# Cross-attention scores of L2 and L3 as 64-row products in two PSUM banks

## What is computed

```python
# L2: biases on q, k, v, o; x is layer-normalised first, the result is added to x
Q = (q @ w_q.T + b_q).reshape(B, Sq, 16, 16).transpose(0, 2, 1, 3)
scores = einsum('bhqd,bhkd->bhqk', Q, K) / sqrt(16)
attn = softmax(scores, axis=-1)
out = einsum('bhqk,bhkd->bhqd', attn, V) -> (B, Sq, 256) @ w_o.T + b_o
# L3: no biases, but a distance bias for each head, a mask, and 1 + sum in the denominator
scores = einsum('bhqd,bhkd->bhqk', Q, K) * scale - slopes[h] * (query_pos - key_pos)
scores = where(mask == 0, -inf, scores)
e = exp(scores - max);  attn = e / (1 + sum(e))
```

## Time and profile before

| | |
|---|---|
| median of 3 runs | 2059.65 us (2058.97 to 2062.86) |
| profiled execution, its own time | 2075.04 us |
| its span, first to last instruction | 2073.2 us |
| mean granted TensorE clock | 0.874 of full speed |
| TensorE busy with products | 1637.2 us, 79% of the span |
| VectorE busy | 1118.5 us, 54% |
| ScalarE busy | 757.3 us, 37% |

### The profile page before, as it was taken

How to read it: one execution, slowest core, us unless ns; L and a number is a source line. 1 busy time by engine, 2 the same in 40 slices (tenths; PEclk the granted TensorE clock), 3 DMA queues, 4 the chain that set the end, 5 groups by cost and what they waited for, 6 DMA issues and landing times. The chain is left out here.

```text
span 2073.2 us, 31829 instructions
## 1 busy us (share of the span) xinstructions
PE 1637.2 (79%) x9560; PEld 1217.6 (59%) x9561; DVE 1118.5 (54%) x2571; ACT 757.3 (37%) x1808; POOL 479.3 (23%) x485
## 2 busy tenths in 40 slices
PE   5965999999999999999998549479544489845993
PEld 4752666666666666666666449358432257634993
DVE  3326565566666666666665620357766846561222
ACT  1211445555445545444542113134344123301331
POOL 1002221222222222222221043211132400006421
PEclk9977999999999999999996569779766589857997
DMA  5001000000000000000003131250100000012203
GB/s 207 0 0 48 1 1 0 0 0 0 0 21 28 1 1 0 0 0 0 1 1 122 41 129 47 96 211 0 31 1 0 0 3 0 0 41 77 64 32 129
DMA packets 25874, 69.19 MB, mean 33 GB/s; under 512 B 6107, under 2 KB 13421, under 8 KB 23756
## 3 DMA queue, kind: packets, MB, share of 16 engines
q1 hardware_dynamic: 19756, 53.35, 7.0%
q0 software_dynamic: 6048, 14.99, 2.3%
HBM read 51.07 MB, written 18.78 MB: 34 GB/s over the span
## 5 line engine op out<-in xcount | busy, mean ns | idle before, releaser
L1062 PE MATMUL banks<-l_ffn_h2T,l_ffn_w 128*128 128x128 f32 (+1 forms) x1536 | 184.0, 278 | 32.2 <-ACT l_ffn_h2T L1175 32.2
L1062 PEld LDWEIGHTS banks<-l_ffn_h2T,l_ffn_w 128*128 128x128 f32 (+1 forms) x1536 | 172.7, 181 | 42.7 <-issue 38.9
L987 PE MATMUL banks<-l_ffn_in_wqkv,l_ffn_hT 128*128 128x512 f32 x384 | 192.2, 611 | 1.9 <-issue 1.1
L1155 ACT ACTIVATE l_ffn_work<-banks,l_ffn_att_bias,l_ffn_att_scale 128x256 f32<-128x256 f32 x256 | 140.5, 567 | 52.2 <-DVE l_ffn_att_bias L1296 52.2
L1009 PE MATMUL banks<-l_ffn_kT,l_ffn_qT 128*128 128x512 f32 x256 | 133.1, 602 | 0.0
L258 POOL TENSOR_TENSOR rstd<-mean_var,neg_half 128x1 f32 (+1 forms) x80 | 46.0, 575 | 350.8 <-DVE mean_var L251 350.7
L1295 DVE TENSOR_REDUCE l_ffn_att_top<-banks 128x2 f32<-128x512 f32 x128 | 88.5, 692 | 62.6 <-PE banks L1009 62.6
L1185 ACT ACTIVATE l_ffn_gate<-banks,l_ffn_layer_cols 128x128 f32<-128x128 f32 x192 | 59.7, 362 | 135.6 <-PE banks L1062 135.6
L1071 PE MATMUL banks<-l_ffn_in_w,l_ffn_ff 128*128 128x256 f32 (+1 forms) x384 | 99.6, 388 | 0.0
L946 POOL TENSOR_TENSOR l_ffn_rden_wide<-l_ffn_att_rden,ones 128x512 f32<-128x512 f32 x32 | 33.2, 1039 | 282.1 <-DVE l_ffn_att_rden L1307 282.1
L2040 DVE COPY l_route_c_all<-l_ffn_in_w 128x1024 f32 x39 | 30.7, 787 | 123.7 <-PE banks L1973 86.9
(11 more groups left out here) (383 smaller groups left out, 3738.6 us busy)
## 6 DMA issues: line engine op xcount, KB each, us to landing
l_experts_rows<-l_experts_pairs SPq DMA_DIRECT2D x16, 512.0 KB, 7.7
l_ffn_in_w<-in_L_w SPq DMA_DIRECT2D x2, 4096.0 KB, 20.4
l_ffn_in_down<-in_L_down SPq DMA_DIRECT2D x1, 4096.0 KB, 14.3
l_experts_c_rows<-l_route_c_all SPq DMA_DIRECT2D x2, 2048.0 KB, 7.6
l_experts_pairs<-l_experts_rows SPq DMA_DIRECT2D x4, 1024.0 KB, 10.5
l_ffn_in_wqkv<-in_L_wqkv SPq DMA_DIRECT2D x1, 3072.0 KB, 12.3
l_ffn_w<-in_L_w SPq DMA_DIRECT2D x2, 1364.0 KB, 7.1
x_res<-in_x SPq DMA_DIRECT2D x4, 512.0 KB, 5.5
```

The lines of the kernel that those rows point to most:

```text
L987: mm = pe.matmul(ps[:, m.bank + 1 + n, :], hT[:, m.b, m.odd, ch, 1 - ch:P + 1 - ch], wqkv[:, bass.ds(m.layer, 1), ch, n * INNER:(n + 1) * ...
L1062: mm = pe.matmul(ps[0:FW[j], m.bank + j // 2, to:to + P], w1[:, ch, at:at + FW[j]], h2T[:, ch, m.b, :], start=(j % 2, n, ch) == (0, 0, 0), ...
L1155: ex = nc.scalar.activation(work[:, m.b, slot, :], ps[:, m.bank + slot // 2, (slot % 2) * 2 * P:(slot % 2 + 1) * 2 * P], ACT.Exp, bias=bia ...
```

## The change

In each half of the channels a group of 64 rows (four heads) becomes a product of its own. Group 0 (partitions 0 to 63) writes bank 4b+2, group 1 (partitions 64 to 127) bank 4b+3; each product has 64 rows, 128 stationary columns and 256 moving columns, and a bank holds 256 columns from each half of the channels. `keys` is half as wide: 4 heads for each row group, selected by `own_quarter`. In L3 the mask and the distance bias are written into both banks first, then the four key products are added. The heads thus stand in another order in the score banks; `head_of` puts the mix back in place, and V1 is laid out to fit.

```diff
+        own_quarter = sb("own_quarter", [P, QUARTER])
-        keys = sb("keys", [P, DCH, BATCH, HALF_XH, CTX])
+        keys = sb("keys", [P, DCH, BATCH, QUARTER, CTX])
...
+                v.tensor_tensor(own_quarter[:], own_head[:, 0:QUARTER], own_head[:, QUARTER:], ALU.add)
...
-                        v.tensor_tensor(keys[:, half, b, :, :], keysT[:, half, b, :].unsqueeze(1).broadcast_to((P, HALF_XH, CTX)),
-                                        own_head[:].unsqueeze(2).broadcast_to((P, HALF_XH, CTX)), ALU.mult)
+                        v.tensor_tensor(keys[:, half, b, :, :], keysT[:, half, b, :].unsqueeze(1).broadcast_to((P, QUARTER, CTX)),
+                                        own_quarter[:].unsqueeze(2).broadcast_to((P, QUARTER, CTX)), ALU.mult)
...
-                    for half in range(2):
-                        r = slice(half * CTX, (half + 1) * CTX)
-                        of = ps[4][r, b * D:(b + 1) * D].rearrange("p (h two x) -> p h two x", two=2, x=XD)[:, :, half, :]
-                        to = V1[r, b, :, half, 0:XD]
+                    for two in range(2):
+                        r = slice(two * CTX, (two + 1) * CTX)
+                        in_heads = lambda ap: ap.rearrange("p (half g a two x) -> p half g a two x", half=2, g=2, a=2, two=2)[:, :, :, :, two, :]
+                        of = in_heads(ps[4][r, b * D:(b + 1) * D])
+                        to = V1[r, b, :, two, 0:XD].rearrange("p (g half a) x -> p half g a x", g=2, half=2)
+                        for half in range(2):
...
-                    for half in range(2):
-                        bank = ps[BANKS * m.b + 2 + half]
-                        mm = pe.matmul(bank, qT[:, m.b, half, :], keys[:, half, m.b, :, :].rearrange("p h n -> p (h n)"), start=True, stop=biased)
+                    for g in range(2):
+                        bank = ps[BANKS * m.b + 2 + g]
                         if not biased:
                             tile = bass.ds(m.it + m.b * TILES, 1)
-                            pe.matmul(bank, e.ident_bf[:], mask[:, tile, :].broadcast_to((P, HALF_XH, CTX)), start=False, stop=False)
-                            mm = pe.matmul(bank, flat(query_rows[:, tile, :]),
-                                           key_rows[:, m.b, half * HALF_XH:(half + 1) * HALF_XH, :].rearrange("p h n -> p (h n)"),
-                                           start=False, stop=True)
+                            pe.matmul(bank, e.ident_bf[:], mask[:, tile, :].broadcast_to((P, HALF_XH, CTX)), start=True, stop=True)
+                            pe.matmul(bank, flat(query_rows[:, tile, :]),
+                                      key_rows[:, m.b, :, :].rearrange("p (half g a) n -> p half g (a n)", half=2, g=2)[:, :, g, :],
+                                      start=False, stop=True, skip_group_check=True)
+                    for half in range(2):
+                        for g in range(2):
+                            own = slice(g * P // 2, (g + 1) * P // 2)
+                            mm = pe.matmul(ps[BANKS * m.b + 2 + g][:, half * D:(half + 1) * D], qT[own, m.b, half, :], flat(keys[own, half, m.b, :, :]),
+                                           start=biased and half == 0, stop=True, skip_group_check=True)
...
-                        mm = pe.matmul(ps[BANKS * m.b + 1][:, j * 2 * (XD + 1):(j + 1) * 2 * (XD + 1)], probsT[:, m.b, j, :], flat(V1[:, m.b, j, :, :]),
+                        to = head_of(j) * (XD + 1)
+                        mm = pe.matmul(ps[BANKS * m.b + 1][:, to:to + 2 * (XD + 1)], probsT[:, m.b, j, :], flat(V1[:, m.b, j, :, :]),
```

More of the change, by code:

```diff
@@ L2161, in cross_attention @@
         sb = memory(e, ctx, name)
-        HALF_XH = XH // 2
+        HALF_XH, QUARTER = XH // 2, XH // 4
+        head_of = lambda pair: pair % 4 // 2 * HALF_XH + pair // 4 * QUARTER + pair % 2 * 2
         wq, wk, wv, wo, own_head = given.wq, given.wk, given.wv, given.wo, given.own_head
         keysT = sb("keysT", [P, DCH, BATCH, CTX])
-        keys = sb("keys", [P, DCH, BATCH, HALF_XH, CTX])
+        own_quarter = sb("own_quarter", [P, QUARTER])
+        keys = sb("keys", [P, DCH, BATCH, QUARTER, CTX])
         qT = sb("qT", [P, BATCH, DCH, P])
@@ L2273, in _ @@
                     for b in range(BATCH):
-                        v.tensor_tensor(keys[:, half, b, :, :], keysT[:, half, b, :].unsqueeze(1).broadcast_to((P, HALF_XH, CTX)),
-                                        own_head[:].unsqueeze(2).broadcast_to((P, HALF_XH, CTX)), ALU.mult)
+                        v.tensor_tensor(keys[:, half, b, :, :], keysT[:, half, b, :].unsqueeze(1).broadcast_to((P, QUARTER, CTX)),
+                                        own_quarter[:].unsqueeze(2).broadcast_to((P, QUARTER, CTX)), ALU.mult)
                 v.wait_ge(s.prep_psum.sem, s.prep_psum.at(0, 2))
                 for b in range(BATCH):
-                    for half in range(2):
-                        r = slice(half * CTX, (half + 1) * CTX)
-                        of = ps[4][r, b * D:(b + 1) * D].rearrange("p (h two x) -> p h two x", two=2, x=XD)[:, :, half, :]
-                        to = V1[r, b, :, half, 0:XD]
[L2282 to L2285, removed]
+                    for two in range(2):
[4 more added lines that the diff above has]
+                        for half in range(2):
+                            if biased:
+                                v.tensor_tensor(to[:, half], of[:, half], in_heads(bv[r, :])[:, half], ALU.add)
+                            else:
+                                v.tensor_copy(to[:, half], of[:, half])
         end(1, s.prep_psum, s.prep_ready)
```

## The result

The changed kernel took 2047.71 us (median of 5 runs, 2044.36 to 2049.48) against 2058.97 us before (5 runs beside it): ratio 0.9945, 95% interval 0.9928 to 0.9963, about 11.3 us less. 20.0 us less were forecast.

The account below looks back on a forecast made before the run. The prediction took TensorE's pace to bound the steady L2 and L3 loops. Its terms, 6.5 + 10.4 + 2.3 + 1.5 - 0.7 = 20.0 us less, gave 2039.6 us, with a range of 2035 to 2052 us.

Parts of the forecast that it names:

- partial overlap: Score products, rival: row groups overlap only in part, 2046.0 us (issue order) or 2051.8 us (weight loads); chance 0.13.
- Row halves run at the same time: Score products: the two row groups overlap fully, four pairs in 0.87 us a tile; chance 0.72.
- The reserve for four groups at 3.07 times the speed: Score pairs: a loss reported for four row groups, if it held, would give back 8 us over 30 tiles.
- Form changes: TensorE: each switch between array forms costs 0.10 us, and the next weights come unhidden.
- L2, 14 steps: L2's steady steps: 0.59 us gained in seven, 0.34 us in seven with a wait at L299; 6.5 us.
- L3, 14 steps: L3's steady steps: scores take 2.42 us for 3.16, 0.74 us less each, nothing late; 10.4 us.
- First tiles of L2: L2's first two tiles, partly at 1.2 GHz: score streams halve, less form costs; 2.3 us less.
- First tiles of L3: L3's first two tiles: the steady 0.74 us gained for each; 1.5 us less.
- Preparation: Key blocks and values' copies: L2 0.7 us later from eight narrower copies, shorter key blocks hidden; L3 0.
- Serial halves: Score products, rival: row groups run one after the other, form changes paid on top; 2066.2 us, chance 0.09.
- no row groups: Score products, rival: 64-row products run in the full form, nothing overlaps; 2060 us, chance 0.03.
- the weights' rival: Score pairs: weights can't load below a running product of the same rows; 1.28 us for pairs, 2051.8 us.

Follow-up runs that it names:

- e4: Changed kernel with VectorE normalising the next input before it weights the mix; ratio to the kernel before 0.9951.
- e13: Kernel before, but L3 issues both masks, then both distance biases, then the full-array keys; ratio to the kernel before 0.9969.
- e2: Changed kernel with L2 computed as before, so only L3 has the new scores; ratio to the kernel before 0.9971.
- e1: Changed kernel with L3 computed as before, so only L2 has the new scores; ratio to the kernel before 0.9984.
- e3: Changed kernel issuing both key products of group 0, then both of group 1, not by turns; ratio to the kernel before 0.9958.
- e8: Changed kernel normalising input before weighting the mix, with GpSimd's L2 bias additions waiting until the mix is weighted; ratio to the kernel before 0.9932.

## Why the prediction was right, and by what it was off

The mechanism of the forecast is right: the two row groups run at the same time, and what was taken from TensorE's step came off the time of the steps. The size is not: 11.3 us came of 20.0. The result lies inside the range partly by luck, since the upper part of the range stood there for partial overlap, and what took the gain was the clock, a wait and first tiles that gave nothing.

**Row halves run at the same time: right.** 1.06 us from scores to transposed mix, of which 1.07 were forecast behind the first change of form. So the column halves of the earlier trace rows were the right stand-in. The reserve for four groups at 3.07 times the speed does not show here: eight records take what four slots take.

**Form changes: right.** The scores start 0.20 us behind the last mix record and not 0.11 (1405.67 against 1403.87 + 1.87 - 0.28 = 1405.46, the last of the 16), as forecast.

**L2, 14 steps, 6.5 us forecast: 5.5 us measured** (13 steps take 80.3 us after, 85.4 before, so 0.39 us a step for 0.465). In the step without GpSimd the forecast had no wait ("just in time"). There was one: the input is ready at 1406.53 + 0.41 = 1406.94 and L299 starts at 1407.07, a handover of 0.13 us and not of 0.06; and behind such a wait the next weights are not hidden, 0.27 us from L299 to the transposed probabilities and not 0.22. The step came to 6.11 and not 5.98. In the other step the size was right (6.26 for 6.23). The forecast had read its 0.06 us off another handover, from the last score record to the maximum. From VectorE to L299 it is 0.13 us in both kinds of step (1400.28 + 0.56 = 1400.84 to 1400.97); from VectorE to L2356 in e4 it is 0.06 us (1400.25 + 0.42 = 1400.67 to 1400.73). So it differs from line to line.

**L3, 14 steps, 10.4 us forecast: 5.9 us in 13 steps.** The step itself was better than forecast, 7.16 for 7.25 us, as a mask takes 0.32 us (1682.14 - 1681.82) and not 0.36. The sum failed at taking 0.74 us for every one of the 14 steps: no engine was late, as forecast, but the clock was not at 1.00 throughout. Three stretches at 1.2 GHz took 4.9 us. "If the clock falls in the steady stretches" stood among what would make the forecast wrong, but no price stood beside it.

**First tiles of L2, 2.3 us less forecast: not shown.** From the first product of the keys to the first transposed mix, in the kernel before, the changed one, e13 and e2 (the last two have L2's old scores; the number behind the counts is the granted clock):

```profile
1354.78:1382.55 27.77, 22.07 (x83) 15.56 (x83) 11.74 (x22) 7.09 (x13) 1.41 (x2) 0.70 0.96 391
1350.10:1375.85 25.75, 19.80 (x94) 16.14 (x95) 10.89 (x27) 7.09 (x13) 1.41 (x2) 0.69 0.99 400
1352.13:1377.04 24.91, 19.04 (x82) 14.00 (x83) 11.75 (x22) 7.10 (x13) 1.41 (x2) 0.82 0.96 388
1350.52:1375.49 24.97, 19.11 (x83) 13.89 (x84) 11.75 (x22) 7.10 (x13) 1.41 (x2) 0.81 0.98 396
```

At the same granted clock, 0.70 and 0.69, the new scores save 2.0 us, and 2.3 without the longer copies: the size forecast. But in two of three traces the old scores have more clock there, 0.82 and 0.81, and take 24.9 and 25.0 us, less than the changed kernel. The new L2 scores take 24.7 to 25.9 us in their eleven traces, at 0.68 to 0.73. So no net gain is shown, and the forecast term held only for a clock that stays as it was.

**First tiles of L3, 1.5 us less forecast: 0.4 us more.** From the first normalisation to the first transposed mix 24.05 us for 23.66. The two score blocks were shorter in work, but more of this stretch ran at half clock (granted clock 0.65 over the 24.05 us, 0.82 over the 23.66 before). How the clock falls there differs between kernels without a pattern that these runs show; this is open.

**Preparation.** L2: copies 1.47 us, 0.18 each, and not 1.84; only 0.3 us later instead of 0.7 (0.64 unrounded), and the 1.52 us in front of them confirm that the shorter key blocks gained nothing. L3: forecast 0, measured 0.4 us more. Its end was set by SyncE, as said. SyncE issues its reloads when the stores have landed, and from the last store's issue to the first reload are 1650.04 - 1647.66 = 2.38 us after the change and 1660.13 - 1658.22 = 1.91 before. Whether the change did that is open: it is 1.9 us in e1, e2 and e13 and 2.4 to 2.7 in the others, and e2 has L3's new scores. Behind it TensorE waited for the last distance-bias transfer to land, which the forecast did not name, but this cost little: L299 starts 1.12 us behind the first normalisation, 1.06 before.

**Rivals.** Serial halves and no row groups are refuted by 1.06 us, and so is the weights' rival, which needed 1.28 us for the pairs alone. Of the partial overlap, the first form said that only neighbours in the order of issue overlap; e3 shows that products need not be neighbours for it. The measured 2047.7 us lies near that rival's 2046.0 us by chance: the steps show full overlap.

## What to carry to other kernels

Row halves that write different banks doubled the speed of products with few rows of contraction here, but each change of array form cost 0.10 us and what weights it uncovered, so put all products of one form side by side. Where a change shortens TensorE's stream, look at the granted clock step by step: this loop kept it always busy and still lost full speed. Compare a stage with more than one trace of the kernel before, as the clock in its first and last tiles moved L2's by 4 us here. And when an input comes just in time, price the handover (0.06 to 0.13 us here) and the unhidden weights behind it, and look for GpSimd work that lies beside VectorE's.

## What the runs showed of the hardware that was not expected

- TensorE granted 1.2 GHz in a loop where its records leave no gap, with five or six form changes in a step of 7.2 or 7.3 us, and 2.4 GHz throughout with two or three in 6.9 us. Whether the changes or the length decide is open.
- Products of a free row group start ahead of earlier issued ones of the busy group (e3: eight records in 1.07 us, and 1.06 us in the order by turns).
- A 128 x 256 float32 normalisation on VectorE took 0.41 us alone, 0.56 us partly beside GpSimd's additions and 0.95 us wholly beside them.
- Two lines in another order and one wait on GpSimd (e8) took 0.19 us off each L2 step on average, with no work removed.
